# A pair's two rounds of products taken apart, and one of three rounding steps moved from POOL to DVE

## The reference

```
goods [2048, 200, 32], cand [2048, 32], W1 [32 + 32 + 1024, 36], b1 [36], W2 [36, 1], b2 [1]
outer  = einsum('bi,bnj->bnij', cand, goods)            # [2048, 200, 32 * 32]
h1     = concat(cand repeated over n, goods, outer)     # [2048, 200, 1088]
act    = sigmoid(h1 @ W1 + b1)                          # [2048, 200, 36]
weight = act @ W2 + b2                                  # [2048, 200, 1]
out    = sum over n of goods * weight                   # [2048, 32]
```

## Time and profile before

| | |
|---|---|
| median of 3 runs | 266.45 us (266.11 to 266.81) |
| profiled execution | 265.84 us, span 264.0 us |
| granted TensorE clock, mean | 0.993 of full speed |
| busy: PE, ACT, POOL, DVE | 252.4, 236.6, 196.8, 193.7 us |
| chain that ended last | PE 91%, ACT 2%, DMA 2%, DVE 2%, POOL 1% |
| goods loads | 256 of 200 KB, median 2.9 us from issue to landing |

### The profile page before, as it was taken

One profiled execution on the slowest core, in us unless ns is written; L12 is line 12 of the kernel. 1 busy time (PEld: TensorE's weight loads), 2 busy tenths in 40 slices (PEclk: granted clock), 3 DMA queues, 4 the chain that ended last, 5 costly groups with the idle time before them and its releaser, 6 DMA issues.

```text
span 264.0 us, 18277 instructions
## 1 busy us (share of the span) xinstructions
PE 252.4 (96%) x7492; PEld 148.1 (56%) x7492; DVE 193.7 (73%) x1108; ACT 236.6 (90%) x658; POOL 196.8 (75%) x349
## 2 busy tenths in 40 slices
PE   7998999999999999999999999999999999999960
PEld 2425656555656656666556566566665565665640
DVE  0890277677778777777777787787787777877886
ACT  2897999999999999999999999999999999999840
POOL 1300787778888888888888888888888888888872
PEclk9999999999999999999999999999999999999997
DMA  5881767767777788777677787787777787777200
GB/s 207 263 298 38 218 190 217 219 203 241 216 227 237 216 240 234 217 235 224 220 237 217 235 230 222 233 233 215 233 226 219 233 233 229 226 222 232 63 0 11
DMA packets 38196, 54.84 MB, mean 208 GB/s; under 512 B 4241, under 2 KB 37905, under 8 KB 38033
## 3 DMA queue, kind: packets, MB, share of 16 engines
q1 hardware_dynamic: 37872, 54.15, 68.1%
q10 hardware_dynamic: 288, 0.32, 0.4%
HBM read 54.19 MB, written 0.26 MB: 206 GB/s over the span
## 4 chain that ended last, share of the span: by engine, by line
PE 91%; ACT 2%; DMA 2%; DVE 2%; POOL 1%; issue 0%; POOLq 0%; DVEq 0%
PE z_ps L337 29%; PE w_ps L384 27%; PE x_ps L360 16%; PE s_ps L422 6%; PE x_ps L422 6%; PE z_ps L289 2%; ACT act L498 2%; DMA act<-w_outer 2%; PE s_ps L337 2%; DVE goods L538 2%; PE s_ps L289 1%; PE x_ps L289 1%; PE x_ps L302 1%; PE w_ps L289 0%; POOL top L255 0%
## 5 line engine op out<-in xcount | busy, mean ns | idle before, releaser
L498 ACT ACTIVATE act<-z_ps,bias 128x200 f32<-128x200 f32 x448 | 149.8, 440 | 10.7 <-PE z_ps L337 4.3
L538 DVE CUSTOM_DVE_ANT_0 goods<-s_ps,goods 128x200 f32<-128x200 f32 x248 | 80.5, 362 | 30.9 <-PE w_ps L422 30.9
L337 PE MATMUL z_ps<-goods,wm_ring 32*32 32x200 f32 x3360 | 78.1, 339 | 0.1
L255 POOL TENSOR_SCALAR top<-whole,consts 128x200 bf16<-128x200 f32 x64 | 50.1, 783 | 21.7 <-DVE whole L530 15.6
L337 PEld LDWEIGHTS z_ps<-goods,wm_ring 32*32 32x32 f32 x3360 | 44.7, 103 | 20.1 <-issue 11.3
L384 PE MATMUL w_ps<-act,consts 128*32 128x200 f32 x1008 | 55.7, 339 | 0.0
L538 DVE CUSTOM_DVE_ANT_0 goods<-x_ps,goods 128x200 f32<-128x200 f32 x124 | 40.4, 364 | 20.6 <-PE s_ps L422 20.6
L360 PE MATMUL x_ps<-goods,wx 128*32 128x200 f32 x1024 | 55.3, 333 | 0.0
L259 POOL TENSOR_SCALAR mid<-rest,consts 128x200 bf16<-128x200 f32 x64 | 50.1, 783 | 6.3
L538 DVE DVE_READ_ACCUMULATOR2_ANT out_stage<- 128x1 f32 x512 | 42.7, 83 | 0.0
L422 PE MATMUL s_ps<-stack,pick_sb 64*128 64x200 bf16 x248 | 42.3, 251 | 0.0
(11 more groups left out here) (53 smaller groups left out, 210.6 us busy)
## 6 DMA issues: line engine op xcount, KB each, us to landing
goods<-goods_t SPq DMA_DIRECT2D x256, 200.0 KB, 2.9
act<-cand_r SPq DMA_DIRECT2D x1, 1024.0 KB, 5.3
act<-cand_u SPq DMA_DIRECT2D x1, 256.0 KB, 2.7
out_t<-out_stage SPq DMA_DIRECT2D x4, 64.0 KB, 2.4
consts<-small ACTq DMA_DIRECT2D x1, 164.5 KB, 5.3
act<-w_outer ACTq DMA_DIRECT2D x1, 144.0 KB, 5.5
pick_sb<-pick SPq DMA_DIRECT2D x1, 128.0 KB, 2.6
```

What stands on the lines that cost most here:

```text
L255: nc.gpsimd.tensor_scalar(top[:, :], whole[:, q % 2, :], m1, None, ALU.mult).then_inc(part_step, 1)
L337: last = nc.tensor.matmul(z_bank(slot, r)[32 * c:32 * c + 32, N * s:N * s + N], weights(slot, 32 * r, 4 * s + c), goods[32 * r:32 * r + 32 ...
L498: last = nc.scalar.activation(act[:, p % A_SLOTS, r, N * s:N * s + N], z_bank(p, r)[:, N * s:N * s + N], ACT.Sigmoid, bias=bias[:, r, p, s ...
L538: last = nc.vector.tensor_tensor_reduce(goods[:, q % G_SLOTS, v, :], s_bank(q, f, s)[:, N * i:N * i + N], goods[:, q % G_SLOTS, v, :], 1.0 ...
```

## The change

- PE's turn is now: first round of products, first spread, second round, second spread, row sums, left-over products. `products` takes the round s as an argument, and only the first round has the waits on goods, on z_read and on the fourth bank's double.
- Banks of the spreads: the first goes to w_ps and s_ps 1, the second to x_ps and the fourth bank's double that the pair before has left. So row sums wait for `pooled[0][0]` of the same turn, left-over products for `pooled[1][0]`, the first round for `pooled[1][1]`; the first spread for `w_kept` and the second for `actx_done`.
- DVE makes top (now double-buffered) right behind whole, and POOL starts from top. In the last turn DVE does both between the two banks of a second spread.
- `wm` is laid out with two neighbouring hidden columns next to each other, and the ring copies move them in twos. The first four pairs' weights go through the ring too, copied by DVE, with biasx after the second.

```
-        wm = sb("wm", [P, UNITS // RUN, HM, RUN])
+        wm = sb("wm", [P, UNITS // RUN, HM // 2, RUN, 2])
-        top = sb("top", [P, N], BF16)
+        top = sb("top", [P, 2, N], BF16)
+        def s_banks(q, f):
+            if q + LAG >= PAIRS:
+                z0, z1, z2, z3 = (z_ps[:, r, :] for r in range(4))
+                return (((z0, z1), (z2, z3)), ((s_ps[1], x_ps), (z0, z1)), ((z2, z3), (s_ps[1], x_ps)))[q + LAG - PAIRS][f]
+            return ((w_ps, s_ps[1]), (x_ps, z_bank(q + LAG - 1, 3)))[f]
         def wm_units(h):
-            return wm[:, :, h, :]
+            return wm[:, :, h // 2, :, h % 2]
+        def of_ring(p):
+            first = p * PAIR_U % RUN
+            units = wm[:, p * PAIR_U // RUN, :, first:first + PAIR_U, :]
+            return (wm_ring[:, p % RING, :, :].rearrange("j u (g e) -> j u g e", e=2),
+                    units.rearrange("j g u e -> j u g e"))
-        POOLED_FROM = [[LAG - 1, LAG - 1], [LAG, LAG]]
+        POOLED_FROM = [[LAG - 1, LAG], [LAG - 1, LAG]]
...
             for q in range(PAIRS):                       # POOL
-                pool.wait_ge(w_kept, q + 1)
-                nc.gpsimd.tensor_scalar(top[:, :], whole[:, q % 2, :], m1, None, ALU.mult).then_inc(part_step, 1)
+                pool.wait_ge(top_made, q + 1)
...
-            def products(p, slot, loaded):
+            def products(p, slot, s, loaded=None):
                 pe.wait_ge(pick_loaded, 16)
+                if s == 0:
+                    pe.wait_ge(goods_loaded[slot % G_SLOTS], loaded)
+                    if slot < FILL:
+                        pe.wait_ge(ring_filled, slot + 1)
+                    if slot >= 1:
+                        pe.wait_ge(z_read, p)
+                    if slot >= LAG + 1:
+                        pe.wait_ge(pooled[1][1], p)
...
             def products_x(p, slot):
...
                 if slot >= LAG:
-                    pe.wait_ge(pooled[0][0], p)
+                    pe.wait_ge(pooled[1][0], p)
...
             def row_sums(p, slot):
...
-                if LAG + 1 <= slot < PAIRS:
-                    pe.wait_ge(pooled[1][1], p)
+                if LAG <= slot < PAIRS:
+                    pe.wait_ge(pooled[0][0], p)
...
                 for slot in range(FILL - 1, FILL - 1 + RING):    # PE's loop body
                     products_x(...)
-                    spread(p, slot, 1)
...
-                    products(p, slot + 1, pe.snap(loaded, ...))
+                    products(p, slot + 1, 0, pe.snap(loaded, ...))
                     spread(p, slot + 1, 0)
+                    products(p, slot + 1, 1)
+                    spread(p, slot + 1, 1)
                     row_sums(p, slot + 1)
...
+            for p in range(FILL):                        # DVE, after its evictions
+                if p == 2:
+                    keep_biasx()
+                nc.vector.tensor_copy(*of_ring(p)).then_inc(ring_filled, 1)
             def keep(p):
...
+                dve.wait_ge(w_kept, KEPT_FROM + p + 1)
+                nc.vector.tensor_scalar(top[:, p % 2, :], whole[:, p % 2, :], m1, None, ALU.mult).then_inc(top_made, 1)
...
                 if q >= 0:
                     pool_units(q, 0)
-                if 1 <= p <= PAIRS:
-                    keep(p - 1)
-                if q >= 0:
-                    pool_units(q, 1)
+                    pool_units(q, 1, PAIRS - 1 if p == PAIRS else None)
+                if 1 <= p < PAIRS:
+                    keep(p - 1)
```

## The result

The changed kernel takes 274.79 us (median of 4 runs, 274.33 to 276.23) against 266.28 for the kernel before beside it: ratio 1.0326, 95% interval 1.0285 to 1.0368. The profiled execution took 274.75, its span is 273.0, against 265.84 and 264.0: the spans differ by 9.0 us.

The account below looks back on a forecast made before the run. It took ACT's loop as the bound, period 3.72 against 3.63: 59 x 0.09 = +5.3 us, less 0.3 at the end, on the profiled 265.84: 270.8, with 0.6 for the median 271.4 us; range 265.0 to 275.0.

Parts of the forecast that it names:

- ACT's loop: Spread, second round, six sigmoids, next first round: 3.62, with 0.10 for a second wait 3.72; taken as bound, +5.3 us.
- the evictions' price: Rival: evictions of wm, written 8 bytes apart, pay half of wxd's price, +3.0 us: 274.4; chance 0.10.
- a period over 3.76: Sign that the forecast of period 3.72 is wrong because a round or a wait is dearer than its row.
- PE without waits: PE's own steps per pair in the new order sum to 3.51 against 3.63, -7.1 us if nothing else waited.
- The second round behind a spread is quick: On PE, the second round, queued behind a spread, takes 0.30 from first to last start instead of 0.60.
- second round stays slow: Rival: PE's second round keeps its 0.60, adding 0.19 to ACT's loop: 276.8 to 282.7 us; chance 0.06.
- DVE's loop: Left-over products wait for six reductions: 3.66, mean 3.68; as the rival that decides, 269.2 us, chance 0.22.
- PE alone: Rival: waits on ACT and DVE don't bind, PE's own 3.51 decides: 259.1 us; chance 0.10.
- both loops at their shortest: Rival: no drain after left-over products (0.68) and one wait only, period 3.62: 265.6 us; chance 0.12.
- Uneven pairs: Time between pairs 4 and 63 beyond 59 regular periods: 1.2 us, left as they are.
- The end: From pair 63's first sigmoid to the last read: 10.8 us instead of 11.12, -0.3 us.
- Parts beside other work: Top on DVE, POOL without it, ring copy, evictions, first four pairs and SP's queue: priced at 0.

Follow-up runs that it names:

- short_inter: Changed kernel with main sigmoids over 100 of 200 columns (output not the reference's) and DVE's reductions reordered to release x_ps one earlier: 259.62 us, ratio 0.9731.
- short: Changed kernel with main sigmoids over 100 of their 200 columns, output not the reference's: 267.04 us, ratio 1.0015.
- inter: Changed kernel with DVE's eight reductions reordered so that x_ps is released one reduction earlier: 275.15 us, ratio 1.0311.
- order: Changed kernel with the first round's wait on pooled[1][1] put ahead of z_read, so z_read sits in the second wait instruction: 270.48 us, ratio 1.0135.
- oiw: Changed kernel with z_read in the second wait instruction, DVE's reductions reordered, and ACT's w_done wait moved ahead of the left-over sigmoid: 266.12 us, ratio 0.9970.
- oi: Changed kernel with z_read in the second wait instruction and DVE's reductions reordered to release x_ps earlier: 269.03 us, ratio 1.0104.
- layout: Kernel before with only the change's weights in twos, ring copies in twos and first four pairs through the ring: 265.76 us, ratio 0.9967.
- topdve: Kernel before, its own PE order, with the change's weight layout and top made on DVE: 266.42 us, ratio 1.0025.
- rlast: Changed kernel with the first round's banks ordered 3, 0, 1, 2, only the last waiting for all sigmoids: 272.90 us, ratio 1.0223.
- ri2: Changed kernel with first-round banks 3, 0, 1, 2, DVE's reductions reordered, and ACT's w_done wait ahead of the left-over sigmoid: 270.35 us, ratio 1.0127.

## Why the prediction held, and where it was off

The forecast was 271.4, and its own range (269.5 to 273.5) lay below the measured 274.79. Against the profiled 274.75 it had 270.8: 3.95 us short. Slower was right, and by ACT's loop. That the wide range (265.0 to 275.0) holds the result is luck: its upper end takes in the evictions' price (274.4), and evictions cost nothing. By the prediction's own sign, a period over 3.76, the forecast as it stood was wrong, since the period is 3.78; what that sign was to mean, a round or a wait dearer than its row, is what happened.

- **PE without waits, 3.51.** Right. In the changed kernel both rounds take 0.56, and short_inter runs at 3.51 with each term at its price; the left-over products keep their 0.79.
- **The second round behind a spread is quick.** Right: 0.30 from first to last start instead of 0.60 (108.43 to 108.70 is the start of the last four, 0.27). The rival "second round stays slow" is out. That it's the queue that makes the difference is argued from this alone; no run held the order and changed the queue.
- **DVE's loop, 3.66, mean 3.68.** Right: 3.64 and 3.71 each third pair in short, hidden in the changed kernel. The rival by which it decides (269.2) failed by its condition: z_read did cost a second wait.
- **ACT's loop as the bound, with a second wait of 0.10.** Right. inter moved nothing, order took 0.10 off the period, and the two wait instructions are 0.106 apart. "PE alone" (259.1) and "both loops at their shortest" (265.6) are out with it.
- **Its size, 3.72.** Too small: 3.784 in the period shown (3.779 is the middle one of the 59). Of my terms, spread 0.28, bank 0.54 (0.546), sigmoids 2.02 and sigmoids to weight load 0.22 (0.218) came out. Two did not. "To ACT's start 0.10" is 0.128: I took it from a place where ACT came from its ring copy with a tie, and called 0.11 the most it could be. Here it waits in earnest, with two conditions. (Matmul ends are modelled; what starts show is 0.67 from second round to first sigmoid, 0.61 in oiw.) "First round 0.56" behind a wait is 0.594 from its first weight load to the next spread, as that load isn't ahead of it (load to matmul 0.03) and the round itself ran 0.57; I had added 0.02 for this to DVE's loop and left it out of ACT's. Together 0.064 a pair, 59 x 0.064 = 3.8 us.
- **Uneven pairs "as they are".** They cost 225.01 - 59 x 3.784 = 1.8 us, where the kernel before had 1.2. 1.3 of the 1.8 are in pairs 4 to 6, whose sigmoids start at 35.65, 40.37 and 44.55. PE's weight loads of the changed kernel in the middle of the first round there:

```profile
38.91 0.14 PEld L342 LDWEIGHTS z_ps<-goods,wm_ring 32*32 32x32 f32 x7 [0.82 <-issue]
```

  PE has nothing to run for 0.82 us in a round that had begun, and no semaphore ends it. Work and waits of that pair are those of all others. What sets it apart is that it is in PE's first passage through the loop body of six turns. The kernel before has such stops too, in pairs 7 and 8, which take 4.08 and 4.15 and hold 1.0 of its 1.2 us; order, oi and oiw have them in these or other early pairs, all before 57 us. The DMA view of the changed kernel has a queue that brings instructions, with six packets between 34 and 60 us and none between 60 and 260, where another one goes on:

```profile
q8 instruction: 6, 0.10, 1.4%
```
```profile
q14 instruction: 19, 0.16, 0.3%
```

  (Packets, MB, share of 16 engines.) So these stops lie where that queue is still at work. That PE waits for its own instructions there is a guess that fits; no run tested it. The difference between the two kernels, 0.6 us of the miss, is one that I didn't forecast and that varies from kernel to kernel.
- **The end, -0.3.** -0.9 to the last read (-0.8 to the end of the span): 10.25 us from pair 63's first sigmoid instead of 10.8, and 11.12 before. Whole and top take 0.69 together and not the 0.9 that I had from whole's row, and the other steps of that sum were each 0.03 to 0.14 too long.
- **Parts beside other work, 0.** Right: layout 0.9967 and topdve 1.0025. The rival on evictions (274.4) is out: 749 ns against 750, although its time is the nearest to the measured one. The Trainium skill's note on SBUF cachelines ("SBUF — State Buffer"), 16-byte lines and full bandwidth from two hits in one, agrees with both: 8 bytes apart is free, and the ring copy fell from 0.71 us to 482 ns.

The balance: 270.8, 3.8 for the two terms of ACT's loop, 0.6 for uneven pairs, 0.1 for the start, -0.5 for the end: 274.8 for 274.75. With the middle period of 3.779 the first two are 3.5 and 0.9.

## What to carry to other kernels

Before giving an engine a better order, close every loop that passes through it and read each term; here the engine's own sum of 3.51 was right to 0.01 and worth nothing, as two other loops closed at 3.64 and 3.78. In a loop that binds, wait instructions are work: put the condition that comes last in the last of them, and give an earlier place to those long met. And don't take a price from a tie as the most that a hand-over can cost: this one was at most 0.11 by the tie and 0.128 once it was waited for.

## What the hardware showed that I had not expected

- A stand-alone wait on PE has 51 ns in the profile and costs 0.106 us more when the awaited semaphore sits in the one before it; swapping the two brought 0.10 a pair (3.78 to 3.68) and 4.3 us of the run (274.79 to 270.48).
- A first round with a wait in its midst, already met, and the banks in another order took 0.65 us in rlast and 0.68 in ri2, where the changed kernel's took 0.57. How much of it is the wait's isn't shown.
- PE stopped for more than 0.3 us in the middle of a round only before 57 us, in the changed kernel (0.82 us at 38.9) as in the others, while a DMA queue that brings instructions was still at work.
- ACT starts 0.128 us after the bank is done when its instruction is preceded by a second condition, long met, and 0.067 when that stands a step earlier: 0.06 a pair, half of what PE's new order was to gain.
